# K, Q and the sum over rows of x times mapped keys as three fp32r products of high and low parts, on one Trainium2 core

## The reference, cut to what matters

```python
xn = _layernorm(x, axis=-1)
# graph layer (1250 nodes, 20000 edges, src and dst)
agg = jax.ops.segment_sum(x[src], dst, num_segments=N)
h = (1.0 + eps) * x + agg                     # then two matmuls with batch norms
# linear attention, feature map elu(t) + 1
q = _feature_map(x @ Wq + bq)
k = _feature_map(x @ Wk + bk)
v = (x @ Wv + bv)
kv = jnp.einsum('bshd,bshe->bhde', k, v)
z = 1.0 / jnp.einsum('bshd,bhd->bsh', q, k.sum(axis=1))
out = jnp.einsum('bshd,bhde,bsh->bshe', q, kv, z) @ Wp + bp
```

## Time and profile before

| | |
|---|---|
| time, median of 3 runs | 597.16 us (596.19 to 597.39) |
| the profiled execution: time, span | 595.98 us, 594.2 us |
| PE busy in the span | 510.9 us (86%) |
| DVE busy | 365.4 us (61%) |
| ACT busy | 247.8 us (42%) |
| POOL busy | 88.8 us (15%) |
| mean granted clock of TensorE | 0.96 |

### The profile page before, as it was taken

The page is one execution under the profiler, slowest core; times in us unless marked ns, Lnnn a source line. Parts: engine busy times, 40 slices in busy tenths (PEclk is TensorE's granted clock), DMA queues, the critical chain, the costliest instruction groups (busy, mean ns, idle before and its releaser), DMA issues.

```text
span 594.2 us, 8244 instructions
## 1 busy us (share of the span) xinstructions
PE 510.9 (86%) x2685; PEld 352.9 (59%) x2685; DVE 365.4 (61%) x1030; ACT 247.8 (42%) x498; POOL 88.8 (15%) x93
## 2 busy tenths in 40 slices
PE   1679999999989999999999999944999999877800
PEld 0334444454579888899999998822454555444400
DVE  4887778767865565378882324973665665644236
ACT  2899777688535442066662223431222222212100
POOL 4001101100000000000000000034344454431210
PEclk9999999999989999999999999967999999999965
DMA  9500000000100019500052006979899999999758
GB/s 308 171 1 2 1 1 1 1 1 2 43 29 0 1 28 381 221 1 2 0 225 95 0 1 258 419 285 411 286 412 416 416 412 416 414 412 406 266 205 341
DMA packets 29432, 108.25 MB, mean 182 GB/s; under 512 B 5019, under 2 KB 6044, under 8 KB 21580
## 3 DMA queue, kind: packets, MB, share of 16 engines
q1 hardware_dynamic: 19148, 88.18, 37.7%
q0 software_dynamic: 5120, 10.26, 4.5%
q10 hardware_dynamic: 5120, 9.26, 4.4%
HBM read 95.58 MB, written 18.63 MB: 192 GB/s over the span
## 4 chain that ended last, share of the span: by engine, by line
PE 73%; DMA 10%; SPq 5%; DVE 4%; issue 4%; ACT 3%; DVEq 0%; POOL 0%; POOLq 0%
PE PS L495 8%; PE PS L494 8%; PE PS L496 8%; PE PS L768 8%; PE PS L783 7%; PE PS L569 6%; PE PS L532 5%; DMA BIG<-in_we 5%; PE PS L524 4%; PE PS L598 4%; PE PS L599 4%; SPq L1468 4%; PE PS L710 3%; PE PS L558 2%; DMA BIG<-y_rows 2%
## 5 line engine op out<-in xcount | busy, mean ns | idle before, releaser
L494 PE MATMUL PS<-ROUND 128*128 128x416 f32 (+3 forms) x232 | 83.7, 361 | 0.0
L495 PE MATMUL PS<-ROUND 128*128 128x416 f32 (+3 forms) x232 | 83.5, 360 | 0.0
L496 PE MATMUL PS<-ROUND 128*128 128x416 f32 (+3 forms) x232 | 83.4, 359 | 0.0
L783 PE MATMUL PS<-BIG 128*64 128x512 f32 x232 | 55.0, 593 | 1.4 <-issue 0.8
L997 DVE BATCH_NORM_STATS2 BST<-BIG 128x6 f32<-128x416 f32 (+1 forms) x36 | 20.7, 590 | 43.8 <-ACT BIG L1334 35.2
L598 PE MATMUL PS<-ROUND 128*128 128x416 f32 (+3 forms) x120 | 44.5, 371 | 2.3 <-DVE ROUND L914 1.8
L494 PEld LDWEIGHTS PS<-ROUND 128*128 128x128 f32 (+1 forms) x232 | 43.5, 188 | 2.6
L496 PEld LDWEIGHTS PS<-ROUND 128*128 128x128 f32 (+1 forms) x232 | 43.6, 188 | 2.5
L898 DVE TENSOR_TENSOR BIG<-PS,BIG 128x280 f32 (+17 forms) x69 | 30.8, 446 | 23.0 <-PE PS L558 18.2
L495 PEld LDWEIGHTS PS<-ROUND 128*128 128x128 f32 (+1 forms) x232 | 43.5, 188 | 2.4
L1181 DVE COPY BIG<-PS 128x512 f32<-128x512 f32 x24 | 16.6, 692 | 45.8 <-PE PS L783 45.8
(11 more groups left out here) (237 smaller groups left out, 904.3 us busy)
## 6 DMA issues: line engine op xcount, KB each, us to landing
BIG<-in_we SPq DMA_DIRECT2D x54, 1024.0 KB
XA<-in_we SPq DMA_DIRECT2D x6, 1024.0 KB
y_rows<-KVB SPq DMA_DIRECT2D x19, 256.0 KB
BIG<-y_rows SPq DMA_DIRECT2D x9, 512.0 KB, 6.6
BIG<-in_we SPq DMA_DIRECT2D x8, 512.0 KB, 13.2
BIG<-in_wqkvp ACTq DMA_DIRECT2D x3, 1024.0 KB, 14.6
XA<-in_x SPq DMA_DIRECT2D x9, 256.0 KB, 10.1
xx_rows<-XA ACTq DMA_DIRECT2D x9, 256.0 KB
```

The source lines that it names most:

```text
L494: mm(o, ah, bh, start=first, stop=False)
L495: mm(o, ah, bl, start=False, stop=False)
L496: return mm(o, al, bh, start=False, stop=last)
L783: ins = mm(PS[64 * j:64 * j + 64, b, :], HT[:, s, 128 * f2 + 64 * j:128 * f2 + 64 * j + 64], buf[:, 1024 + 512 * f2:1024 + 512 * f2 + 512] ...
```

## The change

Every factor of K, of G and of Q is split into a high part (rounded to fp32r) and a low part (what is left, itself fp32r), and `products` takes the place of the plain fp32 matmul.

- The high part of XT comes straight from the PSUM bank (`xth`, ACT, in the place of `xtc`), and the low part by a DVE subtraction from the same bank (`xtl`, new). The low parts lie over XA (`XLR`), tile by tile as `xn` has used it up, and so x is loaded a second time, by SP after the front's use of them.
- The weights: `wkh` rounds WK in four steps on ACT, `wkl` subtracts on POOL; `wq` does both on POOL, four times a copy and a subtraction.
- The mapped keys: `ph` rounds on ACT, POOL subtracts behind its addition to KSUM.
- The low part of XN (`xl`) moves from DVE and the first `agg` round to POOL, right behind `xh` of each tile.
- Plain XT, which `ht` needs, is put together again on POOL in nine additions (step `ks` on POOL) after the last `qmm`; `ht` waits for all nine (`s_xtr`).
- Q has chunks of 512, 512 and 226 columns (`QCH`) instead of `CH`.
- The transfer of WP moves from ACT's queue at the start to SP's, behind WV.
- `begin` is 14.0 instead of 12.0, `unit` 2.4 instead of 2.7, `gmm` is due later behind its tile, `xn` of the last tile earlier.

```diff
+QCH = [(0, 512), (512, 512), (1024, 226)]
...
-    begin, pair, unit, turn = 12.0, 6.0, 2.7, 1.5
+    begin, pair, unit, turn = 14.0, 6.0, 2.4, 1.5
...
+    for k in range(4):
+        at(8.85 + 0.01 * k, "wkh", k)
+        at(9 + 0.01 * k, "wkl", k)
+        at(12 + 0.01 * k, "wq", k)
     for i in range(NT):
         k = begin + pair * i
-        xt = k - (3.0 if i else 1.5)
-        at(xt - 1.2, "xn", i)
+        xt = k - (4.2 if i else 2.5)
+        at(xt - (1.2 if i < NT - 1 else 6), "xn", i)
         at(xt, "xt", i)
-        at(xt + 1, "xtc", i)
+        at(xt + 1, "xth", i)
+        at(xt + 1.7, "xtl", i)
+        at(k + 0.1, "xh", i)
+        at(k + 0.8, "xl", i)
         for q in range(4):
             at(k + pair * q / 8, "kmm", i, q)
-            at(k + pair * (1.45 + q / 8), "gmm", i, q)
+            at(k + pair * (1.7 + q / 8), "gmm", i, q)
         at(k + pair / 2 + 0.3, "kadd", i)
         at(k + pair / 2 + 1.2, "kexp", i)
         at(k + pair / 2 + 2.4, "phi", i)
-        at(k + pair / 2 + 3.2, "xh", i)
-    done = begin + pair * (NT + 0.95)
+        at(k + pair / 2 + 3.0, "ph", i)
...
-            if c == 0:
-                at(base + turn * i - 1.7, "xl", i)
...
+        HTHf, XTH = HTH.bitcast(F32), HTL
+        XTHf = XTH.bitcast(F32)
...
+        PHIL = [rounded(q, 512) for q in (TM0, TM0 + 1024, KK0, KK0 + 512)]
+        PHIH = [rounded(QT0 + 2048 + 512 * q, 512) for q in range(4)]
+        WKL, WQL, WKH, WQH = (by(rounded(q, 2048), 4) for q in (RW0, RW0 + 2048, QT0, OH0))
...
+        def low_part(i, flat):
+
+            if i < 8:
+                return flat[:, 512 * i:512 * i + 512].rearrange("p (k n) -> p k n", k=4)
+            return flat[:, 4096:5000].rearrange("p (k n) -> p k n", k=4)[:, :, 128 * (i - 8):128 * (i - 8) + rows(i)]
+
+        XLR = rounded(END, NT * D)
+        XLF = XLR.bitcast(F32)
...
-                        if i == 0:
-                            pe.wait_ge(sd_w["k"], 16)
                         bank(("k", i))
-                    ins = mm(PS[0:n, b, :], XT[:, k, cs], WK[:, k, :], start=(k == 0), stop=(k == 3))
+                    if i == 0:
+                        pe.wait_ge(s_wl, k + 1)
+                    ins = products(PS[0:n, b, :], XTH[:, k, cs], low_part(i, XLR)[:, k, :], WKH[:, k, :], WKL[:, k, :],
+                                   k == 0, k == 3)
                     if k == 3:
                         ins.then_inc(full[b], 1)
                 elif kind == "gmm":
                     i, k = step[1:]
                     n = rows(i)
                     if k == 0:
-                        pe.wait_ge(s_phi, i + 1)
-                    ins = mm(PS[:, 4 + k, :], XN[0:n, i, 128 * k:128 * k + 128], PHI[i % 4][0:n, :], start=(i == 0),
-                             stop=(i == NT - 1))
+                        pe.wait_ge(s_pl, i + 1)
+                        pe.wait_ge(s_xl, i + 1)
+                    f = slice(128 * k, 128 * k + 128)
+                    ins = products(PS[:, 4 + k, :], XNH[0:n, i, f], XNL[0:n, i, f], PHIH[i % 4][0:n, :], PHIL[i % 4][0:n, :],
+                                   i == 0, i == NT - 1)
...
+                    (o, w), (b, use) = QCH[c], at_of(("q", r, c))
                     f = slice(128 * r, 128 * r + 128)
                     if k == 0:
                         if r == 0 and c == 0:
-                            pe.wait_ge(sd_w["q"], 16)
+                            pe.wait_ge(s_wl, 8)
                         bank(("q", r, c))
-                    ins = mm(PS[:, b, 0:w], WQ[:, k, f], XT[:, k, o:o + w], start=(k == 0), stop=(k == 3))
+                    if c < 2:
+                        xl = XLR[:, 0:4096].rearrange("p (i k n) -> p i k n", i=8, k=4)[:, 4 * c:4 * c + 4, k, :]
+                    else:
+                        xl = XLR[:, 4096 + w * k:4096 + w * k + w]
+                    ins = products(PS[:, b, 0:w], WQH[:, k, f], WQL[:, k, f], XTH[:, k, o:o + w], xl, k == 0, k == 3)
...
-                    if c == 0:
-                        pe.wait_ge(s_xl, i + 1)
...
-                elif kind == "xl":
-                    i, n = step[1], rows(step[1])
-                    dve.wait_ge(s_xh, i + 1)
-                    if i < NT - 1:
-                        dve.wait_ge(s_g, i + 1)
-                    else:
-                        b, use = plan["gts"][3]
-                        dve.wait_ge(full[b], use)
-                    V.tensor_tensor(XNL[0:n, i, :], XN[0:n, i, :], XNHf[0:n, i, :], ALU.subtract).then_inc(s_xl, 1)
+                elif kind == "xtl":
+                    i, n, (b, use) = step[1], rows(step[1]), at_of(("xt", step[1]))
+                    dve.wait_ge(s_xth, i + 1)
+                    if i == 8:
+                        dve.wait_ge(s_xn, NT)
+                    pv = PS[:, b, :].rearrange("p (k n) -> p k n", k=4)[:, :, 0:n]
+                    V.tensor_tensor(low_part(i, XLR), pv, XTHf[:, :, 128 * i:128 * i + n], ALU.subtract).then_inc(moved[b], 1)
...
+                    dve.wait_ge(s_xtr, 9)
...
+                    if i == 0:
+                        dve.wait_ge(sd_xal, 32)
...
-            act.dma_start(WP, wqkvp[3].rearrange("(k p) n -> p k n", p=128)).then_inc(sd_w["p"], 16)
...
-                elif kind == "xtc":
+                elif kind == "xth":
                     i, n, (b, use) = step[1], rows(step[1]), at_of(("xt", step[1]))
                     act.wait_ge(full[b], use)
                     pv = PS[:, b, :].rearrange("p (k n) -> p k n", k=4)[:, :, 0:n]
-                    A.copy(XT[:, :, 128 * i:128 * i + n], pv).then_inc(moved[b], 1)
+                    A.copy(XTH[:, :, 128 * i:128 * i + n], pv).then_inc(s_xth, 1)
+                elif kind == "wkh":
+                    act.wait_ge(sd_w["k"], 16)
+                    A.copy(WKH[:, step[1], :], WK[:, step[1], :]).then_inc(s_wh, 1)
+                elif kind == "ph":
+                    i, n = step[1], rows(step[1])
+                    act.wait_ge(s_phi, i + 1)
+                    A.copy(PHIH[i % 4][0:n, :], PHI[i % 4][0:n, :]).then_inc(s_ph, 1)
...
+                    pool.wait_ge(s_ksum, i + 1)
+                    pool.wait_ge(s_ph, i + 1)
+                    G.tensor_tensor(PHIL[i % 4][0:n, :], u, PHIH[i % 4].bitcast(F32)[0:n, :], ALU.subtract).then_inc(s_pl, 1)
+                elif kind == "wkl":
+                    k = step[1]
+                    pool.wait_ge(s_wh, k + 1)
+                    G.tensor_tensor(WKL[:, k, :], WK[:, k, :], WKH.bitcast(F32)[:, k, :], ALU.subtract).then_inc(s_wl, 1)
+                elif kind == "wq":
+                    k = step[1]
+                    if k == 0:
+                        pool.wait_ge(sd_w["q"], 16)
+                        pool.wait_ge(s_wh, 4)
+                    G.tensor_copy(WQH[:, k, :], WQ[:, k, :]).then_inc(s_wh, 1)
+                    pool.wait_ge(s_wh, 5 + k)
+                    G.tensor_tensor(WQL[:, k, :], WQ[:, k, :], WQH.bitcast(F32)[:, k, :], ALU.subtract).then_inc(s_wl, 1)
+                elif kind == "xl":
+                    i, n, (b, use) = step[1], rows(step[1]), at_of(("xt", step[1]))
+                    pool.wait_ge(s_xh, i + 1)
+                    pool.wait_ge(full[b], use)
+                    G.tensor_tensor(XNL[0:n, i, :], XN[0:n, i, :], XNHf[0:n, i, :], ALU.subtract).then_inc(s_xl, 1)
+                elif kind == "ks":
+                    b, use = at_of(("q", 3, 2))
+                    pool.wait_ge(full[b], use)
+                    for i in range(9):
+                        n = 128 if i < 8 else 226
+                        xs = slice(128 * i, 128 * i + n)
+                        lo = low_part(i, XLF) if i < 8 else by(XLF[:, 4096:5000], 4)
+                        G.tensor_tensor(XT[:, :, xs], XTHf[:, :, xs], lo, ALU.add).then_inc(s_xtr, 1)
...
+            sp.dma_start(WP, wqkvp[3].rearrange("(k p) n -> p k n", p=128)).then_inc(sd_w["p"], 16)
+            sp.wait_ge(s_xtr, 9)
+            sp.dma_start(XA[:, 0:9, :], x_in[0:1152, :].rearrange("(i p) d -> p i d", p=128)).then_inc(sd_xal, 16)
+            sp.dma_start(XA[0:N - 1152, 9, :], x_in[1152:N, :]).then_inc(sd_xal, 16)
```

12 lines of the change are left out of this document (6 added, 6 removed).

## The result

The changed kernel takes **609.74 us**, median of 4 runs (608.01 to 610.82), against 596.67 (594.72 to 597.39) for the kernel before, measured beside it: ratio 1.0222, 95% interval 1.0186 to 1.0257. The forecast was 604 us in a range of 589 to 618, with 0.68 on slower: the time is longer by 13.1 us where 7.3 were added up. The profiled execution took 609.94 us with a span of 607.6.

A forecast was written before the change was run, and what follows sets the result against it. PE was taken to bound the front's last two stages, with DVE bounding the middle after the change. Terms 12.5 + 6.7 - 7.0 - 4.9 = +7.3 us on 595.98 gave 603.3, with the median 1.2 higher 604 us; range 589 to 618.

The forecast's parts named there:

- The signs named for it: DVE over 90% busy from 12 to 115 us, PE gaps in the middle, step ks near 130 us, among others.
- Loss per subtraction, 0.85 us: What DVE loses standing beside each POOL subtraction of 1.27 us; ends 0.40 and 1.04.
- Start, +12.5: 10 to 45.6 us, up to tile 2's exponential: POOL contention and added DVE work; ends +3 and +16.
- The narrower rival of strict alternation: Start: DVE and POOL alternate one to one until about 27 us; sum +10, 607 us; chance counted with the forecast.
- Middle, +6.7: 45.6 to 112.4 us, up to step ks: DVE becomes the bound at 73.5 us; ends -7 and +10.
- Last stage, -7.0: Step ks to last qmm: PE saves 6.0 on Q, 1.0 on three edge groups; nobody else bounds.
- First round, -4.9: First agg round: PE's 3.3 us stand before tile 8 goes, and 1.6 us of lower clock.
- Restoring XT: Nine POOL additions after Q, 12.4 us, at worst 16; ht 16.5 us after last qmm; hidden, no cost.
- Narrow fp32r: Q's 226-column matmuls: 0.11 us each taken; rival 0.38 each, Q 13 us more, 617 or 605 us, chance 0.22.
- The rival in which POOL costs less: Loss of 0.40 per subtraction gives 592 us, no loss 579; chance 0.28 for a faster kernel.
- Behind the front, nothing: After the front: untouched and gated by it; x's second load and WP cost nothing.

The follow-up runs named there:

- run 1: Changed kernel with all 28 POOL subtractions over 8 of 512 columns, matmuls reading the high parts instead: 594.91 us, ratio to before 0.996.
- run 2: Changed kernel with only the tiles' 20 POOL subtractions (PHI and XN) over 8 columns, matmuls reading those high parts: 598.77 us, ratio 1.003.
- run 4: Kernel before with only XN's low parts (xl) moved to POOL in the Q stage, behind Q units: 592.38 us, ratio 0.9929.
- run 5: Kernel before with two more POOL subtractions per tile, into memory that nobody reads: 599.4 us, ratio 1.0038.

## Why the prediction was right

**Direction and mechanism.** Slower, by DVE standing beside POOL: runs 1 and 2 shorten POOL's subtractions and leave order, waits and matmuls, and the time falls by 15 and 11 us. The signs named for it are there: DVE is busy for 97.8 of the 103 us from 12 to 115 us, PE has gaps in the middle, and `ks` comes at 129.6. The size was off: the sum had 7.3 us and the profiled executions differ by 14.0. By its own terms:

- **Loss per subtraction, 0.85 us.** It measured 0.83 in the middle and 0.91 in the start. Right; runs 4 and 5 have 0.29 and 0.5 where DVE has room.
- **Start, +12.5.** It was +15.0. The subtractions were 9.2 of it (60.6 against 51.4), where 11.1 were counted. All else was 5.8, where 1.8 were counted (3.6 of DVE work and 1.2 for the copies on POOL, less the 3 that I let absorb): this part was under-counted most. I counted what DVE had to do and not where the steps came to stand in its order: the exponential of tile 0 was 14 us late, 5.3 of them in DVE's queue behind ready operands. The narrower rival of strict alternation had group 0's one-hots ready 11 us late. They were ready at 19.47 us against 15.68, 3.8 late, since POOL stood for WQ from 16.5 to 18.7; while POOL works, the one-hots and edge operations do take turns with it.
- **Middle, +6.7.** It was +2.4. The DVE time was near the count (68.2 us for 70.5) and DVE waited for 0.8 us and not for 3. With the tiles' subtractions shortened the stage takes 63 us (run 2) and not the 57.3 of PE alone: of the 9.5 us that PE had to win, 5.7 never came, with no engine above 93%. That the order's waits are why is argued, not tried. The stage's bound was right, its floor without contention too low.
- **Last stage, -7.0.** It was -4.5. PE's work fell by 6.0, not 7.0; two groups of edges had gone ahead, not three. The rest is new waiting: the first reciprocal (L945) lies now beside narrow Q units of 1.3 us, and PE stood for the `ata` behind it. That nobody else bounds there was read from means over the stage.

```profile
163.35 2.76 DVE L945 RECIPROCAL XG<-PS 128x418 f32<-128x418 f32 x1
...
166.77 0.46 PE L581 MATMUL PS<-BIG 128*128 128x340 f16 x2 [1.82 <-DVE BIG L923]
```

- **First round, -4.9.** It was -2.7, with the stall gone as said. Here the stand was mis-sized: 3.3 us were read from the chain, which from 170.84 on runs through DVE while PE still works, and the earlier trace rows has PE idle for only 1.8 us. The stand was 2.0 and the lower clock the 1.6 that were counted (rows under run 4), 3.6 together, and run 4, which removes the same stall alone, has -3.3. The new waits for reciprocal and rounding (0.6 and 0.3 us) took back the rest. Restoring XT took POOL 12.36 us and held two of DVE's operations of 226 columns to 1.22 and 1.38 us instead of 0.38; `ht` came 5 us after its end and PE didn't wait.
- **Narrow fp32r.** 0.11 us at 226 columns, as taken; that rival is out. The rival in which POOL costs less is out by the 0.83.
- **Behind the front, nothing.** It was +3.1, between +0.8 and +3.4 in all kernels made from the changed one, against -0.6 and +1.1 in the two made from the kernel before. Nearly all of it lies behind the first matmul of the experts, 183.6 us from the end before and 186.6 in the changed kernel. There the granted clock was 0.50 from 417.9 to 427.9 us (0.71 from 407.5 to 417.5 before). What causes it was not tried, and stays open.

Terms of the front come to +10.2 measured for +7.3 predicted. That 604 is only 6 us off is in part luck: the middle was over-counted by 4.3 us, which hides as much of what start, last stage, first round and the rest were under-counted by (2.5, 2.5, 2.2 and 3.1).

## What to carry to other kernels

Work on an idle GpSimd isn't free: price each of its operations on SBUF at what VectorE loses beside it, here 0.8 to 0.9 us of 1.27 where VectorE is full or has many short operations in a row, and 0.3 to 0.5 where it has a good part of its time over; where VectorE is the bound, its own 0.68 us was cheaper. Take such work to the stage in which another engine is the bound, as run 4 does, which alone beats the kernel before (0.993). And when a due time is shifted in a schedule by due times, look on every engine at what it has passed: here 2 us on one number put 14 small operations, 2.4 us in all, ahead of the one that ACT and PE waited for.

## What was not expected of the hardware

VectorE operations of 0.23 to 0.31 us of work (L837 to L839, 157 columns) take 1.18 to 1.38 us each beside a row of GpSimd subtractions. By these rows the loss goes by the count of instructions, not by their size, so many short ones suffer most. One with an input in PSUM ran at its own length through the same microsecond (L923, 0.31 us at 65.93).
